# The memory stage of a decoder layer: batch by batch, with weight products made beforehand and retrieval with tokens on partitions

## The reference

```
h = relu(y @ scorer_w1.T); scores = sigmoid(h @ scorer_w2.T)
order = argsort(-scores)[:50]                 # per batch, ties by position
pool = (y[order] @ summ_w.T), kept where the score is over 0.5
q = y @ q_w.T;  k = pool @ k_w.T;  v = pool @ v_w.T        # 64, 64, 256 wide
attn = softmax(where(in_memory, q @ k.T * 0.25, -1e9))
retrieved = attn @ v
gate = sigmoid(concat(y, retrieved) @ gate_w.T)
y = y + gate * retrieved * (mean(scores) > 0.3 and count > 0)
```

## Time and profile before

| | us |
|---|---|
| three runs | 888.88, 892.65, 892.62; median 892.62 |
| profiled execution, own time | 893.49 |
| its span | 891.8 |
| TensorE, VectorE, ScalarE, GpSimd busy | 727.9, 459.4, 266.5, 263.2 |
| mean granted clock | 0.873 |

### The profile page before, as it was taken

How to read it: one execution, slowest core, us unless ns; L and a number is a source line. 1 busy time by engine, 2 the same in 40 slices (tenths; PEclk the granted TensorE clock), 3 DMA queues, 4 the chain that set the end, 5 groups by cost and what they waited for, 6 DMA issues and landing times.

```text
span 891.8 us, 14179 instructions
## 1 busy us (share of the span) xinstructions
PE 727.9 (82%) x4918; PEld 543.5 (61%) x4919; DVE 459.4 (52%) x991; ACT 266.5 (30%) x501; POOL 263.2 (30%) x243
## 2 busy tenths in 40 slices
PE   1996664699999858577869879999967399999996
PEld 1842221467667623343336668888767399999995
DVE  5378898565656465622441345454532644444441
ACT  1355455122222123012221334535341022222221
POOL 2723565667776560030000000000000112222221
PEclk9997797699999879568895799999985589999999
DMA  5000000111111119000000000000039000111110
GB/s 179 1 0 0 0 0 0 54 49 40 53 35 56 33 50 376 1 0 0 0 3 1 0 1 20 13 20 14 20 113 331 12 26 31 35 33 31 35 32 1
DMA packets 36218, 37.87 MB, mean 42 GB/s; under 512 B 4647, under 2 KB 32620, under 8 KB 36172
## 3 DMA queue, kind: packets, MB, share of 16 engines
q1 hardware_dynamic: 32956, 32.11, 11.0%
q0 software_dynamic: 2208, 5.12, 2.0%
q10 hardware_dynamic: 1008, 0.03, 0.1%
HBM read 26.77 MB, written 5.11 MB: 36 GB/s over the span
## 4 chain that ended last, share of the span: by engine, by line
PE 59%; issue 17%; DVE 12%; POOL 5%; ACT 4%; DMA 1%; POOLq 0%; SPq 0%; DVEq 0%; ACTq 0%
PE quad L1838 9%; PE bank L1849 9%; PE bank L1609 4%; PE bank L1693 4%; DVE arena L898 3%; PE quad L1424 3%; PE quad L1707 3%; PE bank L1742 2%; PE bank L1746 2%; PE quad L1728 2%; POOL arena L422 2%; PE bank L1733 2%; PE bank L1802 1%; PE bank L1399 1%; DVE ybuf L998 1%
## 5 line engine op out<-in xcount | busy, mean ns | idle before, releaser
L1424 PE MATMUL quad<-featT,ybuf 128*128 (+1 forms) x128 | 66.2, 676 | 25.1 <-DVE arena L887 24.7
L1849 PE MATMUL bank<-arena,prob_b 128*128 x368 | 83.1, 379 | 0.0
L1838 PE MATMUL quad<-ybuf 128*128 128x128 f32 x560 | 81.1, 281 | 0.0
L898 DVE SCALAR_TENSOR_TENSOR arena<-arena,conv_w 128x512 f32<-128x512 f32 x72 | 71.5, 1055 | 10.7 <-ACT arena L603 10.7
L1838 PEld LDWEIGHTS quad<-ybuf 128*128 128x128 f32 x560 | 74.7, 198 | 1.1
L1849 PEld LDWEIGHTS bank<-arena,prob_b 128*128 128x128 f32 x368 | 68.2, 190 | 8.4
L1424 PEld LDWEIGHTS quad<-featT,ybuf 128*128 128x128 f32 x128 | 27.6, 219 | 62.3 <-issue 35.2
L1176 DVE TENSOR_REDUCE ybuf<-quad 128x8 f32<-128x1232 f32 x32 | 46.0, 1436 | 31.0 <-PE quad L1707 30.8
L789 ACT ACTIVATE prob_b<-quad,gate_w 128x128 f32<-128x128 f32 x92 | 26.4, 368 | 117.4 <-PE quad L1838 117.4
L538 POOL DMA_INDIRECT out<-featT,dts x23 | 23.3, 1015 | 123.1 <-DVE featT L1356 123.1
L518 POOL TENSOR_TENSOR xres<-xres,ybuf 128x256 f32 x16 | 11.6, 724 | 156.1 <-DVE ybuf L1196 156.1
(11 more groups left out here) (351 smaller groups left out, 1538.6 us busy)
## 6 DMA issues: line engine op xcount, KB each, us to landing
arena<-W1T SPq DMA_DIRECT2D x8, 1024.0 KB, 12.0
arena<-W2T SPq DMA_DIRECT2D x8, 1024.0 KB, 12.0
arena<-arena SPq DMA_DIRECT2D x16, 384.0 KB, 3.1
xres<-x SPq DMA_DIRECT2D x4, 512.0 KB, 6.6
x_rows<-xres SPq DMA_DIRECT2D x16, 128.0 KB, 1.7
ybuf<-attn_in_wT SPq DMA_DIRECT2D x1, 1288.0 KB, 11.6
featT<-b SPq DMA_DIRECT2D x8, 128.0 KB, 5.0
w_out<-attn_out_wT SPq DMA_DIRECT2D x1, 512.0 KB, 12.7
```

Source lines behind the costliest of these rows:

```text
L898: i = dve.scalar_tensor_tensor(acc, raw[:, g, k:k + BLK], conv_w[:, g, k:k + 1], acc, ALU.mult, ALU.add)
L1424: m = pe.matmul(bank[f % 5][:, :], w_in[:, k, f * P:(f + 1) * P], featT[:, k, ds(blk * BLK, BLK)], start=(k == 0), stop=(k == KD - 1))
L1838: m = pe.matmul(bank[2 * p + half][:, f * P:(f + 1) * P], w1_now[k][p][:, (4 * half + f) * P:(4 * half + f + 1) * P], xsT[:, p, k, :], sta ...
L1849: m = pe.matmul(bank[4 + p][:, 0:D], hidT[:, p, f, :], w2_of[:, ds(e * NFF + f, 1), :].rearrange("p a n -> p (a n)"), start=(f == 0), stop ...
```

## The change

Scoring: y is scaled half on VectorE and half on ScalarE, batch by batch, the scorer of one batch writes two blocks to the two halves of the PSUM partitions, the relu goes to ScalarE, and the score columns are one-column transposes. Ranks: the triangle of the own tile is part of the comparison. While batch 0 is ranked, TensorE multiplies the weights with each other: w_key (summary, key and query weights), w_val (summary and value weights) and w_vgate (these and the gate's lower half), so that keys, values and the values' part of the gate come straight from the 50 selected rows. The order is then batch 0, the attention keys with the ranks of batch 1 between them, the attention values, batch 1, and the retrieval of 8 pairs of tiles with tokens on partitions: one product of y with [upper half of the gate | keys] gives gate part and logits in one PSUM bank, and the retrieved values and their gate part come from the turned attention weights. GpSimd adds the update to the residual. The normalised rows of batch 0 are made and turned within the last two pairs. A root of a constant on ScalarE ahead of the last chunks loads its table.

```diff
@@ ScalarE
+            act.activation(red[:, 0, 0:1], eps_col[:, :], ACT.Sqrt)
...
+            def keep_memory(b):
+                act.wait_ge(S("select_mm"), b + 1)
+                act.activation(pool_tokT[:, b, :, :], bank[4 + b][:, P:2 * P].rearrange("p (k n) -> p k n", k=KD)[:, :, 0:POOL], ACT.Copy
+                               ).then_inc(S("pool_tokT_ready"), 1)
+                act.wait_ge(S("key_mm"), b + 1)
+                act.activation(side_w[:, :, b, D:GW], bank[4 + b][:, 2 * P:3 * P].rearrange("p (k n) -> p k n", k=KD)[:, :, 0:POOL], ACT.Copy,
+                               scale=0.25).then_inc(S("side_ready"), 1)
...
+            exp_logits(0)
+            for n in range(NT // 2):
+                if n:
+                    tanh_gates(n - 1)
+                if n == 5:
+                    row_sd2(0)
+                if n >= 6:
+                    norm_rows(2 * n - 12, (4 * n - 24, 4 * n - 23))
+                    norm_rows(2 * n - 11, (4 * n - 22, 4 * n - 21))
+                keep_attnT(n)
+                if n >= 6:
+                    keep_hT(2 * n - 12)
+                if n + 1 < NT // 2:
+                    exp_logits(n + 1)
+                if n >= 6:
+                    keep_hT(2 * n - 11)
@@ VectorE
+            for n in range(NT // 2):
+                if n:
+                    gate_values(n - 1)
+                if n + 1 < NT // 2:
+                    soften_start(n + 1)
+                if n:
+                    row_stats2(n - 1)
+                if n + 1 < NT // 2:
+                    soften_end(n + 1)
+                if n:
+                    row_vars2(n - 1)
...
@@ GpSimd
+            for n in range(NT // 2):
+                pool.wait_ge(S("upd_ready"), n + 1)
+                xv = xres[:, 2 * n:2 * n + 2, :].rearrange("p a d -> p (a d)")
+                pool.tensor_tensor(xv, xv, upd[:, n % 2, :], ALU.add).then_inc(S("x1_ready"), 1)
@@ TensorE
+            def select(b):
                 pe.wait_ge(S("onehot_ready"), b + 1)
-                for k in range(TB):
-                    pe.matmul(mem_bank[b][1][0:POOL, 0:D], onehot[:, b * TB + k, :], y_tok[:, b * TB + k, :], start=(k == 0), stop=(k == TB - 1))
...
+                for c in range(KD):
+                    for k in range(TB):
+                        m = pe.matmul(bank[4 + b][:, P + 64 * c:P + 64 * c + POOL], y_tok[:, b * TB + k, c * P:(c + 1) * P],
+                                      onehot[:, b * TB + k, :], start=(k == 0), stop=(k == TB - 1))
...
+            for k in range(TB):
+                keys_of(k)
+                rank_cols(1, k)
...
+            def head(n):
+                b, x0 = n // (NT // 2 // B), 2 * (n % 3)
+                pe.wait_ge(S("side_ready"), B + b + 1)
+                if n >= 3:
+                    pe.wait_ge(S("gate_tanh"), n - 2)
+                for i in range(2):
+                    for k in range(KD):
+                        m = pe.matmul(bank[x0 + i][:, 0:GW], featT[:, k, (2 * n + i) * P:(2 * n + i + 1) * P], side_w[:, k, b, :],
+                                      start=(k == 0), stop=False, skip_group_check=True)
+                m.then_inc(S("logit_mm"), 1)
...
+            def retrieve(n):
+                b, x0 = n // (NT // 2 // B), 2 * (n % 3)
+                pe.wait_ge(S("attnT_ready"), n + 1)
+                pe.wait_ge(S("vals_ready"), b + 1)
+                if n:
+                    pe.wait_ge(S("upd_ready"), n)
+                for i in range(2):
+                    at_ = attnT[0:POOL, n % 2, i * P:(i + 1) * P]
+                    pe.matmul(bank[x0 + i][:, 0:D], at_, vals[0:POOL, b, D:2 * D], start=False, stop=True, skip_group_check=True)
+                    m = pe.matmul(bank[6][:, i * D:(i + 1) * D], at_, vals[0:POOL, b, 0:D], start=True, stop=True)
+                m.then_inc(S("gate_mm"), 1)
...
+            head(0)
+            select(1)
+            memory_sides(1)
+            pe.wait_ge(S("vals_ready"), B)
+            for n in range(NT // 2):
+                if n + 1 < NT // 2:
+                    head(n + 1)
+                turn_attn(n)
...
+                retrieve(n)
```

More of the change, by code:

```diff
@@ L1513, in _, with turn_y @@
             total_square(NT - 1, 1)
[L1515 to L1519 removed]
+            def turn_y(n):
+                pe.wait_ge(S("y_even"), n + 1)
+                pe.wait_ge(S("y_odd"), n + 1)
+                if n >= 4:
+                    pe.wait_ge(S("yT_dve" if n % 2 else "yT_act"), n // 2 - 1)
+                for t in (2 * n, 2 * n + 1):
@@ new lines, in mean_scores, with rank_cols @@
+            def mean_scores(b):
+                pe.wait_ge(S("s_col_ready"), 2 * b + 2)
+                pe.matmul(bank[4 + b][:, 16:16 + 2 * TB], ones[:, :], s_valid[:, b, :, :].rearrange("p a t -> p (a t)"), start=True, stop=True
+                          ).then_inc(S("mean_mm"), 1)
+            def rank_cols(b, k):
+                if k == 0:
+                    pe.wait_ge(dve_once, at("ones_bf_set_1"))
+                pe.wait_ge(S("rank_counted"), b * TB + k + 1)
+                for j in range(k, TB):
+                    m = pe.matmul(bank[2 + b][:, j:j + 1], greater[:, k % 2, j * P:(j + 1) * P], ones_bf[:, 0:1],
+                                  start=(k == 0 and j == 0), stop=(k == j), skip_group_check=True)
+                m.then_inc(S("rank_cols"), 1)
@@ new lines, in _ @@
+            for n in range(4):
+                turn_y(n)
+            pe.wait_ge(S("mem_w_loaded"), 16 * 8)
+            score_hidden(0)
+            turn_y(4)
+            turn_y(5)
+            turn_y(6)
+            turn_y(7)
+            pe.wait_ge(dve_once, at("w2b_ready"))
+            score_rows(0)
+            score_hidden(1)
+            turn_scores(0)
+            score_rows(1)
+            mean_scores(0)
+            rank_cols(0, 0)
+            summ, q_nat = w_nat[0:SD, 0, :], w_nat[0:SD, 1, :]
@@ new lines, in _ @@
+            for k in range(KD):
+                m = pe.matmul(bank[0][:, k * D:(k + 1) * D], mem_v_w[:, k * P:(k + 1) * P], summ, start=True, stop=True)
+            m.then_inc(pe_once, reached("w_mm_2"))
+            for k in range(KD):
+                m = pe.matmul(bank[1][:, k * D:(k + 1) * D], summ[:, k * P:(k + 1) * P], mem_v_w[:, :], start=True, stop=True)
+            m.then_inc(pe_once, reached("w_mm_3"))
+            rank_cols(0, 3)
+            rank_cols(0, 4)
+            pe.wait_ge(act_once, at("w_made_3"))
@@ new lines, in _, with keys_of @@
+            select(0)
+            memory_sides(0)
+            mean_scores(1)
+            def keys_of(n):
+                b, g = n // NG, n % NG
+                if n >= 2:
+                    pe.wait_ge(S("keys_ready"), n - 1)
+                for k in range(KD):
+                    pe.matmul(bank[6 + n % 2][:, 0:LK], wk_pad[:, k, g * P:(g + 1) * P], ctxT[:, b, k, :], start=(k == 0), stop=False)
+                pe.matmul(bank[6 + n % 2][:, 0:LK], mask_sel[:, :], mask_row[:, b * LK:(b + 1) * LK], start=False, stop=True
+                          ).then_inc(S("keys_mm"), 1)
@@ L1684, in _ @@
+            for n in range(4, 8):
+                turn_rows2(n)
+            pe.wait_ge(S("hT_ready"), 6)
+            pe.wait_ge(S("hT_ready_dve"), 2)
+            pe.wait_ge(S("pads_zero"), 7)
             pe.wait_ge(S("key_tail_ready"), GH)
```

752 lines of the change are left out of this document (365 added, 387 removed).

## The result

| | before | after |
|---|---|---|
| median of four executions in one session, us | 890.75 | 849.13 |
| profiled execution, own time | 893.49 | 848.82 |
| its span | 891.8 | 847.1 |
| mean granted clock | 0.873 | 0.883 |
| last column of squares to first query product | 187.10 | 140.44 |

The account below looks back on a forecast made before the run. It took the chain of waits from last column of squares to first query, 187.1 us, as the bound. Seven pieces summed to -26.2: 893.49 becomes 867.3, 866 as median, range 846 to 886.

Parts of the forecast that it names:

- the root's table load off the path: Between last column of squares and scorer: the square root's table loads earlier, in ScalarE's idle time; the load is 1.28 us.
- half products that overlap: Scorer: two blocks on different halves of the array run together, 3.5 us at the low clock, 7 if they don't.
- TensorE as the end of the ranks at the low clock: Ranks of batch 0: TensorE's weight products end at 351.7 at the low clock, behind VectorE's sweep at 342.9; 348 was taken.
- batch 1's ranks under the keys: Attention keys hide the whole ranking of batch 1; up to 8 us would come back if that failed, chance 0.02.
- the last piece: Last norms and turns, from the last pair to the first query: 9.8 us against 12.7, -2.9.
- Piece 2: Scorer products to score columns: 21.9 us becomes 13.7, -8.2.
- Piece 6: Attention keys and values, with batch 1's rank columns between: 29.7 us becomes 34.7, +5.0.
- Piece 4's second half: Selection and sides of batch 1, behind the keys: 18.8 us, with selecting products at the low clock.
- Piece 5: Retrieval, now eight pairs of tiles: 73.2 us becomes 49, -24.2, first pair at the low clock, seven at the high.
- The rival of a high clock already in the weight products and both selections: Clock high already for weight products, both selections and first pair: 25 us less, 841; chance 0.12.
- half of the pairs would run low: Retrieval: the clock sinks again and again in the pairs, +14 us, 880; chance 0.18.
- the interference of GpSimd with the triangle operations: Ranks of batch 0: eight triangle products wait up to 0.77 us each; VectorE would end at 349 instead of 342.9.

Follow-up runs that it names:

- the reordered kernel: Changed kernel with last weight products behind the rank columns, batch 1's score turns behind batch 0's selection, normalised rows behind attention weights: 848.73 us median, ratio 0.944.

## Why the prediction was wrong in size

Right in the forecast: the root's table load off the path; half products that overlap (eight records in 1.94 us, where one after another at 0.43 would be 3.4); TensorE as the end of the ranks at the low clock; 7.0 for the 7.7 us of the first selection; pairs 5.28 us apart for 5.3, seven of them at the high clock (the first seven, where the forecast had the last seven); batch 1's ranks under the keys; the last piece within 0.5.

The step that failed is the clock at which three pieces were priced. They came out 19.1 us below their terms, and 18.5 are missing in all (the others nearly cancel). Most of the 19.1 is clock, not all:

- Piece 2 was taken at the low clock, since the scorer of the kernel before starts so. It starts so behind turns of y that came slowly: the clock went down at about 321 amid them, and then TensorE was idle for 5.90 us. The change leaves 1.64 us idle ahead of the turns and 0.88 ahead of the scorer. I had counted the early root as 1.3 us. The run without it shows that it also decides the scorer's clock: 4.8 in all up to the selection. At the high clock TensorE no longer ends this piece: the path is a table load (1.28), tanh (1.09) and halving (1.15), of which tanh and halving were put beside TensorE's products and the load was in no term.
- Piece 6 was taken at the low clock, by the row 468:496 of the earlier trace rows. That row was read as "dense and low", and what makes it low was not asked. The one-row products take 0.81 of the 2.13 us of a key there (470.67 to 471.48):

```profile
470.67 0.88 PE L1660 MATMUL bank<-w_out 1*128 1x154 f32 x2
471.48 1.40 PE L1659 MATMUL quad<-arena 128*128 128x154 f32 x4
```

That they decide the clock is shown for the new kernel; in the kernel before it was not tried. The new stage enters the keys behind products of 256 columns with the clock just up, and the keys then let it sink after five, or in one profile not at all. In the run with all rank columns first, where every key ran at the low clock, keys and values took 31.7 us (362.42 to 394.11), about 33.3 with the rank columns. So 5.7 of the 7.1 are clock, and 1.4 other terms: the rank columns and the mean were put at 3.7, and the eight rank columns took 1.6.
- Piece 4's second half was taken low because the ranks stood ahead of it in the kernel before. Here the values and the head product (L1747, 3.92 us) do, the clock comes up at 392, and the products of selection and sides take 6.5 us instead of 13.

Piece 5 hides the same error twice. The first pair was taken low at 10 us and took 5.36 at the high clock; the last was taken high and ended at the low one, some 9 us. With 46.4 for 49 the two nearly cancel, which is luck.

The rival of a high clock already in the weight products and both selections (841) came true in the second selection and the first pair only; the weight products ran at 0.50 in every profile looked at for it, but for parts of a few us. That half of the pairs would run low (880) did not come true; in the first profile only the last was hit, whose attention weights wait for rows of batch 0 on ScalarE (2.07 us from 439.36).

Two smaller terms: the interference of GpSimd with the triangle operations was there, 0.11 us in the mean of the sixteen where I had allowed up to 0.77 for eight of them, and hidden by TensorE. The Trainium skill (SBUF — State Buffer, Who interferes with whom) says that an operation with two SBUF inputs waits for GpSimd and the accumulating scalar form doesn't; the traces agree, 464 against 350 ns and 1144 against 1142. The table load took 1.28 us with the root 0.02 behind it again, in the run without the early root; the drain of the Trainium skill (ScalarE: Activation LUTs, What ACT_TABLE_LOAD costs) isn't seen.

I had left out that the first queries would start at the low clock, since TensorE waits in the tail: the first takes 3.54 us for the 2.07 of the earlier trace rows, and with it all behind the stage takes 2.4 us more.

What stays open: why one execution of the same program keeps the clock through the keys and another doesn't, and what picks between the two starts of the stage, 312 and 317. The runs show that both differ with the same instructions, not what picks one. Whether the single row of weights is what counts against the clock, or any added product would do the same, is open as said above. Why the weight products run low is open too: spare products did not cure it. That the first pair of the reordered kernel ran low was seen in one of its two profiles (and in the run with the shortened additions), and its cause was not tried.

## What to carry to other kernels

When a term of the sum is a stretch of TensorE, price it at both clocks and ask what stands in it, not whether it is busy: here a busy stretch turned slow with products that use one row of weights in it, and stayed quick without them. Bias and mask rows folded into products look cheap (0.45 us for a mask row at the high clock), but moved out and added by an idle engine they gave 17 us against the slower executions of the changed kernel and 5 against the quicker. Half of an expected gain can be luck, too: an edit of order that seemed to give the 6 us expected owed 3 of them to a selection that ran at the high clock in that profile. And a program whose clock has two states at one place needs several profiles before an edit of 5 us can be judged by its time.

## What the runs showed of the hardware

- The clock can sink while TensorE is never idle: 4.00 of 4.00 us busy in 368:372 at 0.54, and 12.00 of 12.00 at 0.50 with the mask row three times, whereas the keys and values without one-row products, busy for 9.93 of 12.04 us, stayed at 1.00. It can also stay up while TensorE is never idle: 16.00 of 16.00 us at 1.00 in 336:352 of the kernel before. The Trainium skill (TensorE: Matmul & The Clock Gate, HAM oscillation — how this bites in real kernels) names idle gaps of TensorE as what costs the clock. The run without the early root agrees with that (idle for 2.80 us for 1.64, and 0.50 in 316:320 for 1.00); the keys don't.
- One program's executions fell in two groups, 833 to 839 and 848 to 851, on one chip in one session; with twelve one-row products moved, in another session, six executions were one group, 829 to 836.
- Two scorer products of 64 output columns each on different halves of the array's columns run together: 1.94 us for eight records of 512 columns at the high clock.
